# Graph attention with layer norm: the order of VectorE's moments, x and reciprocals changed, and the edges of the adjacency found on GpSimd

## The reference

```
q, k, v = split_heads(x @ Wq + bq), split_heads(x @ Wk + bk), split_heads(x @ Wv + bv)
scores  = q @ k^T / sqrt(32) + beta * adj        # per graph and head, 256 x 256
scores  = where(adj > 0, scores, -9e15)
out     = softmax(scores) @ v                    # heads put together again, 256 x 384
result  = layernorm(x + out)                     # over the 384 features, eps 1e-5
```

## Time and profile before

| what | value |
|---|---|
| median of 3 runs | 659.75 us (659.65 to 660.05) |
| the profiled execution's own time | 659.83 us |
| its span in the profile | 658.0 us |
| mean granted clock of PE | 0.981 |
| busy PE, DVE, ACT, POOL | 610.0, 592.2, 578.5, 407.0 us |
| one turn in the middle | about 19.1 us |

### The profile page before, as it was taken

How to read it: one execution, slowest core, us unless ns; L and a number is a source line. 1 busy time by engine, 2 the same in 40 slices (tenths; PEclk the granted TensorE clock), 3 DMA queues, 4 the chain that set the end, 5 groups by cost and what they waited for, 6 DMA issues and landing times. The chain is left out here.

```text
span 658.0 us, 20660 instructions
## 1 busy us (share of the span) xinstructions
PE 610.0 (93%) x6056; PEld 488.6 (74%) x6056; DVE 592.2 (90%) x2320; ACT 578.5 (88%) x2058; POOL 407.0 (62%) x642
## 2 busy tenths in 40 slices
PE   5999999999999999999999999999999999999841
PEld 4877787877878778787777878777787777778520
DVE  2899999999999999999999999999999999999625
ACT  4899999999999999999999999999999999999711
POOL 3333427777666677766667776666777666677633
PEclk9999999999999999999999999999999999999866
DMA  6259778998887889888888987878898888877701
GB/s 188 78 121 204 172 163 188 208 215 172 194 194 177 207 197 223 172 194 191 194 188 191 225 180 189 194 186 194 189 221 184 192 194 190 192 163 176 185 25 72
DMA packets 68223, 118.15 MB, mean 180 GB/s; under 512 B 10512, under 2 KB 36368, under 8 KB 68112
## 3 DMA queue, kind: packets, MB, share of 16 engines
q1 hardware_dynamic: 67024, 116.63, 76.5%
q10 hardware_dynamic: 1088, 0.20, 0.2%
HBM read 22.94 MB, written 12.58 MB: 54 GB/s over the span
## 5 line engine op out<-in xcount | busy, mean ns | idle before, releaser
L442 ACT ACTIVATE probs<-neg_scores,neg_max 128x256 f32<-128x256 f32 x768 | 383.5, 505 | 3.0 <-DVE neg_max L524 2.9
L524 DVE CUSTOM_DVE_ANT_0 neg_scores<-s_bank,bias_sb 128x256 f32<-128x256 f32 x768 | 280.0, 418 | 27.3 <-PE s_bank L408 18.8
L558 DVE STREAM_TRANSPOSE blocks<-probs 128x512 f32<-128x512 f32 x310 | 198.0, 685 | 0.0
L442 ACT ACTIVATION_READ_ACCUMULATOR probs<-neg_scores,neg_max 128x1 f32 x768 | 151.6, 197 | 0.0
L458 ACT ACTIVATE qk<-j_bank,qk_bias 128x256 f32<-128x256 f32 x192 | 90.1, 469 | 40.1 <-PE j_bank L332 37.0
L408 PE MATMUL s_bank<-qk 32*128 32x256 f32 x1536 | 110.0, 399 | 13.7 <-DVE neg_max L524 13.0
L332 PE MATMUL j_bank<-xt_high,w_high 128*128 128x256 f32 x576 | 112.4, 303 | 1.6 <-ACT w_high L473 1.6
L408 PEld LDWEIGHTS s_bank<-qk 32*128 32x128 f32 x1536 | 71.0, 184 | 54.2 <-ACT v_sb L460 37.2
L361 PE MATMUL j_bank<-shuffled,v_sb 128*32 128x256 f32 x1240 | 100.9, 390 | 9.5 <-issue 8.8
L750 POOL TENSOR_SCALAR att<-att,rstd,shift 128x384 f32<-128x384 f32 x60 | 99.0, 1656 | 6.5 <-POOL shift L747 6.5
L332 PE MATMUL j_bank<-xt_high,w_low 128*128 128x256 f32 x576 | 99.3, 281 | 0.0
(11 more groups left out here) (57 smaller groups left out, 893.0 us busy)
## 6 DMA issues: line engine op xcount, KB each, us to landing
shuffled<-blocks SPq DMA_DIRECT2D x496, 160.0 KB, 4.1
x_sb<-in_x_dram SPq DMA_DIRECT2D x32, 384.0 KB, 5.5
out_dram<-att SPq DMA_DIRECT2D x30, 384.0 KB, 5.5
adj_sb<-in_adj_dram SPq DMA_DIRECT2D x32, 256.0 KB, 5.3
out_dram<-att SPq DMA_DIRECT2D x4, 192.0 KB, 2.1
blocks<-in_L_gnn_Wq_dram SPq DMA_DIRECT2D x1, 576.0 KB, 5.8
blocks<-in_L_gnn_Wk_dram SPq DMA_DIRECT2D x1, 576.0 KB, 8.4
blocks<-in_L_gnn_Wv_dram SPq DMA_DIRECT2D x1, 576.0 KB, 9.5
```

The costliest lines, as they stand in the source:

```text
L442: nc.scalar.activation(probs[:, (T * s + t) % (T * NX), :], neg_scores[:, (T * s + t) % (T * NH), :], ACT.Exp, bias=neg_max[:, n % 2, t, h ...
L524: nc.vector.tensor_tensor_reduce(neg_scores[:, (T * s + t) % (T * NH), :], s_bank[h % J][:, t * N:(t + 1) * N], bias_sb[:, n % 2, t, :], - ...
L558: nc.vector.transpose(blocks[:, n % 2, :, h, :, :].rearrange("p k t q -> p t k q"), probs[:, slot:slot + T, :].rearrange("p t (k q) -> p t ...
```

## The change

Four things. The `edges` of a graph go from DVE to POOL, in front of what `bias` did there; POOL waits for the adjacency and for the maxima of the graph that used the slot before. `moments` go from h = 9 to h = 11 of a turn (in the last turn they stay at h = 4). At h = 9, DVE takes the job X behind the maxima of the next graph's head 0 and ahead of those of its head 1. The row sums of a graph are inverted at once, at h = 0 of the next turn (for the last graph still group by group), and the wait of G counts accordingly.

```diff
@@ take(job) on DVE, job G
-                    dve.wait_ge(inv_ready, G * n + a + 1)
+                    dve.wait_ge(inv_ready, n + 1 if n < B - 1 else n + a + 1)
@@
             def invert(n, g):
-                dve.wait_ge(exp_ready, T * (H * n + J * (g + 1)))
-                nc.vector.reciprocal(inv_sum[:, n % 3, :, J * g:J * (g + 1)],
-                                     row_sum[:, n % 2, :, J * g:J * (g + 1)]).then_inc(inv_ready, 1)
-
-            def edges(n):
-
-                dve.wait_ge(adj_in, (n + 1) * DMA)
-                nc.vector.tensor_scalar(bias_sb[:, n % 2, :, :], adj_sb[:, :, :], 0.0, MASKED,
-                                        ALU.is_le, ALU.mult).then_inc(not_edge_ready, 1)
+                heads = slice(0, H) if g is None else slice(J * g, J * (g + 1))
+                dve.wait_ge(exp_ready, T * (H * n + heads.stop))
+                nc.vector.reciprocal(inv_sum[:, n % 3, :, heads], row_sum[:, n % 2, :, heads]).then_inc(inv_ready, 1)
@@ DVE's order (edges(0) and edges(1) ahead of the loop are taken out too)
                     if h % J == 1:
-                        for ahead in (s + 3, s + 4):
-                            if ahead < B * H:
-                                maxima(ahead)
+                        if s + 3 < B * H:
+                            maxima(s + 3)
+
+                        if h != 2 * J + 1 and s + 4 < B * H:
+                            maxima(s + 4)
                         for job in jobs_of(n, h):
                             take(job)
+                        if h == 2 * J + 1 and s + 4 < B * H:
+                            maxima(s + 4)
@@
-                    if h == 11 and n + 2 < B:
-                        edges(n + 2)
-                    if h % J == 0:
-                        if h > 0:
-                            invert(n, h // J - 1)
-                        elif n >= 1:
-                            invert(n - 1, G - 1)
-                    if h == (4 if n == B - 1 else 9) and n >= 3:
+                    if h == 0 and n >= 1:
+                        invert(n - 1, None)
+                    elif h % J == 0 and n == B - 1:
+                        invert(n, h // J - 1)
+                    if h == (4 if n == B - 1 else 11) and n >= 3:
                         moments(n - 3)
@@ bias(n) on POOL
+                pool.wait_ge(adj_in, (n + 1) * DMA)
+                wait(pool, max_ready, T * H * (n - 1))
+                nc.gpsimd.tensor_scalar(bias_sb[:, n % 2, :, :], adj_sb[:, :, :], 0.0, MASKED,
+                                        ALU.is_le, ALU.mult).then_inc(not_edge_ready, 1)
                 pool.wait_ge(not_edge_ready, n + 1)
+                take_wait()
                 nc.gpsimd.tensor_scalar(adj_sb[:, :, :], adj_sb[:, :, :], 0.0, beta_col[:, 0:1],
                                         ALU.max, ALU.mult).then_inc(adj_beta_ready, 1)
```

More of the change, by code:

```diff
@@ L638, in _ @@
             weights_low(0)
-            edges(0)
             weights_low(1)
@@ L646, in _ @@
                 take(job)
-            edges(1)
             for n in range(B):
```

## The result

The changed kernel takes 703.57 us (median of 4 runs, 702.22 to 704.77) against 659.76 us before: ratio 1.0668, 95% interval 1.0655 to 1.0681. The forecast was 699 us, range 682 to 714. The ratios in this document leave out one execution, a slower one of 668.92 us among the twelve of a_moments, in which the granted clock was lower too (0.973).

What follows compares the result with a forecast made beforehand. A loop from DVE's head 0 through moments, POOL's layer_norm, edges and bias was to set 20.46 us a turn. 93.7 us to the first moments, 552.4 for 27 turns and 51.2 of tail, plus 1.8, gave 699 us, range 682 to 714.

Steps and rivals of the forecast that it cites:

- The slack of 3.25 us: Before the change, POOL's bias ends at 314.40 us and DVE takes head 0 at 317.65 us.
- The loop's terms: DVE from head 0 through moments 5.34 us, signal 0.24, layer_norm 9.08, edges 2.19, rest of bias 3.49, signal 0.12: 20.46.
- The edges on POOL: The 128x512 edges instruction on POOL was taken at 2.01 us, plus 0.18 us of wait for its result.
- Rivals 1 and 2: POOL's edges at 0.42 us, 656 us, chance 0.05; or at 0.6 to 1.2 us, 661 to 677 us, chance 0.06.
- The run's terms: First moments end at 93.7 us, 27 turns take 552.4, tail 51.2, execution lies 1.8 over its span.
- It just fits: At the start, POOL's first bias is ready at 16.5 us; DVE's first maxima start at 16.58 us.
- The signs: DVE waits 1.4 to 2 us for bias each turn, moments 20.4 us apart, POOL's edges near 2.0 us.
- SP's queue: Adj load, store and x load come later by 4 us or so, still ahead of the next 16 shuffles.
- Up to 0.8 us: Moments filling DVE's hole at the turnaround could save this a turn, if nothing else ruled; PE allows 0.4 at most.
- the floor of 18.66 us of PE work: PE has 18.66 us of work in a 19.10 us stretch, taken as the least a turn could take.
- 4 (no wait): DVE's wait for bias isn't there, the order being misread; 0.4 us a turn kept, near 649 us, chance 0.03.
- 3 (the clock): PE's clock falls in the new pause; at half clock for 6 us a turn takes 21.7 us, 732 us, chance 0.07.

Runs made afterwards that it cites:

- a_moments: The kernel before with one edit, moments at h = 11 instead of h = 9: 662.67 us, ratio 1.0040.
- b_edges: The kernel before with only the edges moved from DVE to POOL: 660.71 us, ratio 1.0016.
- ax: The kernel before with moments at h = 11, add_residual ahead of layer_norm and x loaded ahead of adj: 653.15 us, ratio 0.9898.
- f_bias_first: The changed kernel with bias(n+2) ahead of layer_norm(n-3) on POOL: 644.03 us, ratio 0.9761.
- e_double: The changed kernel with the edges instruction issued twice on POOL: 758.88 us, ratio 1.1501.
- g_x_early: The changed kernel with add_residual ahead of layer_norm on POOL and x loaded ahead of adj: 700.41 us, ratio 1.0617.
- f_h9: The changed kernel with bias ahead of layer_norm on POOL and moments back at h = 9: 661.98 us, ratio 1.0035.

## Why the prediction was right, and where its steps were off

**What bounds it: right.** The slack of 3.25 us in the loop from the moments through layer_norm and bias to head 0, against 4.5 us added, was the whole case. b_edges (2.2 us added) and ax (2.3 us added) each stay inside the slack, both together don't (ax barely: DVE waits for bias in half of its turns), and f_bias_first, which only takes bias out of the loop, turns +6.7% into -2.4%. e_double shows the one-for-one.

**The loop's terms: right.** Forecast 5.34, 0.24, 9.08, 2.19, 3.49, 0.12, sum 20.46; measured 5.29, 0.28, 9.08, 2.15, 3.48, 0.17, sum 20.45.

**The edges on POOL: right.** Taken as L708's 2.01 us, measured 1.94 us over 32 times. The comparison costs POOL no more than the max did. The Trainium skill, page GPSIMD Engine Reference, section Elementwise — side-by-side cycle accounting, gives 769 ns for 512 elements as a best case, of a tight loop; the trace shows 2.5 times that for this two-operation instruction. Rivals 1 and 2 were built on such speeds, and the trace refutes them.

**The run's terms.** Moments (3) end at 94.6 us instead of 93.7: in this execution the adjacency landed at 11.9 us, not at 10.85, and DVE waited 3.83 us for the first bias. "It just fits" held only for the earlier landing. The 27 turns took 555.2 us instead of 552.4, 20.56 on average. The tail was 50.6 us, forecast 51.2. The median of the runs lies 1.4 us above the profiled execution. The four differences, 0.9 + 2.8 - 0.6 + 1.4, are the 4.5 us between forecast and result.

**The signs.** DVE's wait for bias was to be 1.4 to 2 us in each of 27 turns. It is there in 24 of them, 2.1 us on average. In the other three (head 0 at 172.77, 275.41 and 378.36 us) DVE waits 0.4 to 0.5 us for the scores instead, each time 12 to 14 us behind a wait of PE for x of 2.4 to 2.8 us; the first of these turns is that of 22.26 us. POOL's wait for the moments is about 2.15 us, as forecast.

**SP's queue: wrong.** The prediction had the load of x "still ahead of the next 16 shuffles", which is true, and stopped there. It should have gone on to who waits for x. In the kernel before, the load was issued at 316.31 us and PE turned this x at 324.29 without a wait, 8.0 us later. In the changed kernel it is issued at 318.40 us and PE turns this x at 323.68, after waiting 1.16 us:

```profile
318.40 0.37 SPq L265 DMA_DIRECT2D x_sb<-in_x_dram  x1
```

```profile
323.68 0.41 PE L341 MATMUL j_bank<-ident,x_sb 128*128 128x128 f32 x2 [1.16 <-DMA x_sb<-in_x_dram]
```

Most of it hid behind DVE's wait for bias; g_x_early puts the rest at 3.2 us by the medians. Between the two profiled executions it is 1.65 us, and the 27 turns of g_x_early still take 553.7 us. So only about half of the 2.8 us that the turns took too long is late x. The other half is still there in g_x_early: in four of its turns one wait between two instructions of POOL takes 0.47 us where it otherwise takes 0.18 to 0.20, and these turns are 0.3 us longer. What makes these waits longer is open. In a_moments, where little waiting for bias hides it (5.8 us in all), it cost 9.5 us (a_moments against ax).

**What DVE's edits are worth: right in the mechanism, too small.** "Up to 0.8 us" a turn for the hole, "PE lets it lose 0.4 at most". f_h9 against f_bias_first shows the full 0.8 us (19.17 to 18.35). The step that failed is the floor of 18.66 us of PE work, taken from the busy time of a stretch: the same matmuls fit in a turn of 18.35 us in f_bias_first. The Trainium skill, page Trainium Kernel Development and Optimization, section Performance Expectations, calls matmul busy time a bad metric for how close a kernel is to its limit, because matmuls are pipelined; the trace agrees. Here the floor entered only the rivals: the 650 us of the first and the 649 us of the fourth would have been lower.

**The rivals.** 1 and 2 (cheap edges on POOL) and 4 (no wait) are refuted by the rows above. 3 (the clock) happened in part: the mean granted clock between 100 and 200 us is 0.98, where it was 1.00. The prediction had called a clock under 1.00 in the middle a sign of being wrong. It wasn't one: the usual turn is still 20.43 us, and the last section shows a stretch.

## What to carry to other kernels

The idle time of an engine doesn't tell how much slack there is for work whose result a loop waits for. Before moving work into it, follow the first instruction behind the new place to the one that waits for it, go round until the path closes, and compare the sum with the period: here 3.25 us of slack took either edit, not both. If the sum is too long, look first at the order on the engine in between: swapping two calls on POOL was worth 60 us, more than all edits on DVE together. And follow each queue behind a moved wait to its consumer, also when the DMA is still issued in order.

## What the runs showed of the hardware

TensorE's granted clock fell in g_x_early's middle while the time did not suffer. PE's pauses, which in the changed kernel were often split in two, one of them for x, now come together. Busy time by stretch of g_x_early (length, PE, PEld, DVE, ACT, POOL; then the granted clock):

```profile
314.40:316.40 2.00, 0.08 (x1) 0.11 (x2) 1.44 (x6) 0.96 (x4) 2.00 (x2) 1.00 0.22 29
316.40:318.40 2.00, 2.00 (x12) 2.00 (x13) 2.00 (x10) 2.00 (x8) 1.13 (x2) 0.81 0.83 294
318.40:322.40 4.00, 4.00 (x38) 1.92 (x37) 2.91 (x12) 2.89 (x11) 1.72 (x6) 0.67 0.59 150
```

PE is still for 2.14 us, then the granted clock is between its two levels on average: part of the time 1.2 GHz, part 2.4. Its mean over the run is 0.959 against 0.977 in the changed kernel, and PE is busy 10.6 us longer (620.1 against 609.5) for the same matmuls. In e_double, where DVE's waits for bias are about twice as long in total (105.2 us against 55.1), the mean is 0.947. The extra PE time lies inside the 20.45 us of the loop.

A load that lands just in time goes with an uneven time. Eleven of the 12 runs of a_moments spread by 8.0 us (658.22 to 666.22), the 4 of ax, which differs only in what loads x earlier, by 1.2 us (652.57 to 653.72). That the load causes the spread is argued from this one pair; only one run of each has a trace.
